# Two PSUM banks for du*B, one for the transposes, three slots of h, and pair sums only on GpSimd, in a fused Mamba and attention kernel

## What is computed

```python
x = whitening of the four channel groups                       # L0, folded into one 128x128 matrix m0
# L1: Mamba block. Per image, L = 1024 positions, 256 inner channels d, 16 states n
delta = softplus(dt @ W_dt + b_dt)
h_t = h_{t-1} * exp(delta_t * A[d, n]) + (delta_t * u_t)[d] * B_t[n]
y_t = sum_n h_t[d, n] * C_t[n];   y = (y + xc * Dp) * silu(z);   x = y @ W_out + x
# L2: attention with softmax over 1024 positions, out = gamma * (v @ softmax(q.k)) + x
# L3: a second softmax attention on theta and phi, convolution, batch norm over all images, + x
```

## Time and profile before

| | us |
|---|---|
| median of 3 runs | 5648.49 |
| lowest and highest | 5642.84, 5652.95 |
| the profiled execution | 5654.98 |
| its span | 5653.2 |

### The profile page before, as it was taken

The page is one execution under the profiler, slowest core; times in us unless marked ns, Lnnn a source line. Parts: engine busy times, 40 slices in busy tenths (PEclk is TensorE's granted clock), DMA queues, the critical chain, the costliest instruction groups (busy, mean ns, idle before and its releaser), DMA issues.

```text
span 5653.2 us, 61917 instructions
## 1 busy us (share of the span) xinstructions
PE 4649.7 (82%) x17331; PEld 2705.2 (48%) x17331; DVE 5067.2 (90%) x5978; ACT 3709.2 (66%) x6077; POOL 4724.3 (84%) x3342
## 2 busy tenths in 40 slices
PE   6568888888888888888888888888888888888871
PEld 6135554455445444545444455445445544554450
DVE  4699999999999999999999999999999999999933
ACT  3456677667766766676677667766666776677633
POOL 0698999999989889898989998989889899999910
PEclk9689999999999999999999999999999999999995
DMA  4456656655655565555556665665566566656517
GB/s 132 176 224 224 224 208 223 229 222 216 224 224 215 215 225 217 216 219 225 223 207 224 224 225 217 222 220 212 219 224 223 210 221 229 224 208 224 219 74 301
DMA packets 199100, 1216.87 MB, mean 215 GB/s; under 512 B 27881, under 2 KB 28657, under 8 KB 67697
## 3 DMA queue, kind: packets, MB, share of 16 engines
q1 hardware_dynamic: 194416, 1196.26, 57.4%
q10 hardware_dynamic: 4352, 16.78, 0.7%
HBM read 1158.43 MB, written 54.53 MB: 215 GB/s over the span
## 4 chain that ended last, share of the span: by engine, by line
PE 38%; DVE 22%; ACT 14%; issue 13%; POOL 10%; DMA 1%; DVEq 0%; SPq 0%; POOLq 0%; ACTq 0%
PE psA L814 13%; PE psE L814 11%; DVE hs L488 8%; DVE psD L484 7%; PE psT L814 7%; POOL pa L300 5%; PE psT L987 4%; ACT da L680 4%; ACT p L726 3%; DVE nm L513 3%; PE psY L814 2%; POOL pa L306 2%; POOL pa L310 1%; ACT L649 1%; ACT pt L690 1%
## 5 line engine op out<-in xcount | busy, mean ns | idle before, releaser
L300 POOL TENSOR_TENSOR pa<-hs,rows_all 128x1024 f32<-128x1024 f32 x1024 | 2412.8, 2356 | 396.8 <-DVE hs L488 396.5
L680 ACT ACTIVATE da<-delta,neg_a 128x512 f32<-128x512 f32 x2048 | 1382.1, 719 | 288.3 <-DVE hs L488 276.2
L484 DVE TENSOR_TENSOR psD<-rows_all,psU 128x512 f32<-128x512 f32 x2048 | 1416.5, 692 | 84.7 <-POOL hlast L304 6.3
L306 POOL TENSOR_TENSOR pa<-pa 128x512 f32<-128x512 f32 x1024 | 1317.1, 1286 | 40.2
L488 DVE TENSOR_TENSOR_SCAN hs<-da,hlast,psD 128x512 f32<-128x512 f32 x1024 | 1310.9, 1280 | 36.3
L488 DVE TENSOR_TENSOR_SCAN hs<-da,psD 128x512 f32<-128x512 f32 x1024 | 1249.4, 1220 | 35.2
L814 PE MATMUL psA<-pt,va 128*128 128x256 f32 x4096 | 989.5, 391 | 71.2 <-DVE x L531 43.7
L814 PEld LDWEIGHTS psA<-pt,va 128*128 128x128 f32 x4096 | 770.0, 194 | 295.5 <-DVE x L531 77.1
L513 DVE TENSOR_REDUCE nm<-psE 128x1 f32<-128x1024 f32 x512 | 620.1, 1211 | 201.1 <-PE psE L814 198.8
L726 ACT ACTIVATE p<-psE,nm 128x1024 f32<-128x1024 f32 x512 | 571.5, 1116 | 316.8 <-DVE nm L513 316.7
L690 ACT ACTIVATE pt<-psT 128x512 f32<-128x512 f32 x1024 | 555.5, 596 | 304.4 <-PE psT L987 301.0
(11 more groups left out here) (186 smaller groups left out, 5017.6 us busy)
## 6 DMA issues: line engine op xcount, KB each, us to landing
rows_all<-bc_scratch SPq DMA_DIRECT2D x1024, 1024.0 KB, 4.7
xin<-x SPq DMA_DIRECT2D x40, 512.0 KB, 7.7
xres<-x SPq DMA_DIRECT2D x64, 256.0 KB, 6.1
x_scratch<-x SPq DMA_DIRECT2D x32, 512.0 KB, 4.3
f_scratch<-fa SPq DMA_DIRECT2D x32, 512.0 KB, 6.8
xres<-x SPq DMA_DIRECT2D x8, 512.0 KB, 3.6
x1g<-x SPq DMA_DIRECT2D x8, 512.0 KB, 3.7
fa<-x SPq DMA_DIRECT2D x8, 512.0 KB, 3.7
```

The costliest lines, as they stand in the source:

```text
L300: pool.tensor_tensor(pa[:, k % PROD, :, :], hs[:, sl, :, :], rows_all[:, slot, 2:4, :], ALU.mult).then_inc(S["prod"], 1)
L306: pool.tensor_tensor(pa[:, k % PROD, 0, :], pa[:, k % PROD, 0, :], pa[:, k % PROD, 1, :], ALU.add).then_inc(S["pair"], 1)
L484: dve.tensor_tensor(psD[:, :], rows_all[:, slot, j, :], psU[:, :], ALU.mult).then_inc(S["dbu_ok"], 1)
L680: act.activation(da[:, k % 2, j, :], delta[:, h, cols(ch)], ACT.Exp, scale=neg_a[:, h, 2 * q + j:2 * q + j + 1]).then_inc(S["da_ok"], 1)
```

## The change

The diff, cut to its core:
- **psD** has two banks; VectorE does both multiplies of a step, then both scans. The copy to psU moves to the end of the group before (`inputs`).
- **hs** has three slots in place of two; VectorE waits for the product two steps back and not for the one of the step before.
- **GpSimd** stops at the pair. TensorE's `add` sums one pair's block at every step, which is 32 sums per image in place of 16, and GpSimd waits for the sum four steps back.
- **psA** is now the second bank of psT. All transposes, the centring and variance, xi of h=0, and the two pre-activations of delta go through the first bank, four transposes at a time, each four waiting until ScalarE has copied the last; xi of h=1, the rows and the weighing go through the second. The gates z use both in turn, h=1 first.
- The keys go through psE. `project` and `project_values` become `query`, `key` and `values` a step later, and x times m0 (`resx`) is taken out of `residual` and put ahead of its wait.

SP's list is unchanged. Wherever ScalarE reads a bank that moved, its line follows.

```diff
@@ buffers and semaphores
+HRING = 3
-        hs = sb("hs", [128, 2, 2, CH])
+        hs = sb("hs", [128, HRING, 2, CH])
-        psD = ps("psD", [128, CH])
+        psD = ps("psD", [128, 2, CH])
         psT = ps("psT", [128, 2, CH])
-        psA = ps("psA", [128, CH])
+        psA = psT[:, 1, :]
-            hlast_ok=STEPS // 2, prod=STEPS, pair=STEPS, quad=STEPS // 2, quad_mm=STEPS // 2, g_ok=2 * NCH,
+            hlast_ok=STEPS // 2, prod=STEPS, pair=STEPS, sum_mm=STEPS, g_ok=2 * NCH,
-        AT_C, AT_N, AT_X, AT_Z, AT_B, AT_P = 0, 3, (5, 7), 9, 10, 11
+        AT_C, AT_N, AT_X, AT_Z, AT_B, AT_P = 0, 3, (5, 6), 9, 10, 11
@@ GpSimd, products
-                    sl, slot = k % 2, k % RING
+                    sl, slot = (b * STEPS + k) % HRING, k % RING
-                    wait(pool, "quad_mm", b, k // 2 - 1)
+                    wait(pool, "sum_mm", b, k - PROD + 1)
...
-                    if k % 2:
-                        wait(pool, "pair", b, k + 1)
-                        pool.tensor_tensor(pa[:, k % PROD, 0, :], pa[:, (k - 1) % PROD, 0, :], pa[:, k % PROD, 0, :], ALU.add
-                                           ).then_inc(S["quad"], 1)
@@ VectorE: scans becomes inputs, spread_inputs, scan_state
+                def inputs(b, k):
+                    ch, h = divmod(k // PAIRS, NH)
+                    wait(dve, "du_ok", b, k // PAIRS + 1)
+                    wait(dve, "dbu_ok", b, 2 * k)
+                    dve.tensor_copy(psU[:, :], du[:, h, cols(ch)]).then_inc(S["u_ok"], 1)
+                def spread_inputs(b, k):
+                    slot = k % RING
+                    if k % PAIRS == 0:
+                        wait(dve, "u_ok", b, k // PAIRS + 1)
+                    at(dve, f"rl{slot}", (b * (STEPS // RING) + k // RING + 1) * 16)
+                    for j in range(2):
+                        wait(dve, "h_ok", b, 2 * (k - 1) + j + 1)
+                        dve.tensor_tensor(psD[:, j, :], rows_all[:, slot, j, :], psU[:, :], ALU.mult
+                                          ).then_inc(S["dbu_ok"], 1)
-                def scans(b, k, j):
+                def scan_state(b, k, j):
                     if j == 0:
-                        at(dve, f"rl{slot}", (b * (STEPS // RING) + k // RING + 1) * 16)
-                        wait(dve, "prod", b, k - 1)
-                        wait(dve, "hlast_ok", b, min(k - 1, NS))
-                    wait(dve, "h_ok", b, 2 * k + j)
-                    dve.tensor_tensor(psD[:, :], rows_all[:, slot, j, :], psU[:, :], ALU.mult).then_inc(S["dbu_ok"], 1)
+                        wait(dve, "prod", b, k - HRING + 1)
+                        wait(dve, "hlast_ok", b, min(k - HRING + 1, NS))
                     wait(dve, "dbu_ok", b, 2 * k + j + 1)
                     wait(dve, "da_ok", b, 2 * k + j + 1)
-                    dve.tensor_tensor_scan(hs[:, sl, j, :], da[:, sl, j, :], psD[:, :],
+                    dve.tensor_tensor_scan(hs[:, sl, j, :], da[:, k % 2, j, :], psD[:, j, :],
@@ VectorE, image
                             if scan:
-                                scans(b, k, 0)
+                                spread_inputs(b, k)
                             if front_of and r == AT_N:
                                 normed(*front_of)
+                            if scan:
+                                scan_state(b, k, 0)
+                            if scan and k % PAIRS == PAIRS - 1 and (k < STEPS - 1 or more):
+                                inputs(*((b, k + 1) if k < STEPS - 1 else (b + 1, 0)))
...
                             if scan:
-                                scans(b, k, 1)
+                                scan_state(b, k, 1)
@@ ScalarE
-                        for h in range(NH):
-                            wait(act, "z_mm", fb, 2 * fc + h + 1)
+                        for n, h in enumerate((1, 0)):
+                            wait(act, "z_mm", fb, 2 * fc + n + 1)
...
-                    if r == AT_P:
-                        for h in range(NH):
+                    if r in (AT_P, AT_P + 1):
+                        h = r - AT_P
...
                             act.activation(pt[:, i // GT % 2, 4 * q:4 * q + 4, 128 * (t % GT):128 * (t % GT) + 128],
-                                           psT[:, q, :].rearrange("p (j i) -> p j i", j=4), ACT.Copy
+                                           psT[:, 0, :].rearrange("p (j i) -> p j i", j=4), ACT.Copy
...
-                        act.activation(ka[:, :], flat(psT), ACT.Identity, bias=c_bk).then_inc(S["k_ok"], 1)
+                        act.activation(ka[:, :], flat(psE), ACT.Identity, bias=c_bk).then_inc(S["k_ok"], 1)
@@ TensorE
-                    if what == "gates":
+                    if what in ("gates1", "gates0"):
+                        h = int(what == "gates1")
+                        wait(pe, "xi_ok", fb, 2 * fc + 2)
+                        if att and h == 1:
+                            wait(pe, "v_ok", *att["valued"])
+                        if att and h == 0:
...
+                        mm(psT[:, h, :], w_in_t[:, DI + C * h:DI + C * h + C],
...
-                    if what == "steps":
+                    if what in ("steps0", "steps1"):
...
                         else:
+                            wait(pe, "sp_abs", fb, 2 * fc + 1)
+                            wait(pe, "sp_relu", fb, 2 * fc + 1)
+                        mm(psT[:, 0, :], w_dt_t[BCR:BCR + DR, C * h:C * h + C], rows_out[BCR:BCR + DR, :]
+                           ).then_inc(S["dpre_mm"], 1)
...
                     if what == "rows":
                         wait(pe, "xc_ok", fb, 2 * fc + 2)
-                        wait(pe, "xi_ok", fb, 2 * fc + 2)
+                        wait(pe, "z_ok", fb, 2 * fc + 1)
...
-                    if q == 1:
+                    if q == 0:
                         wait(pe, "g_ok", b, group)
-                    if k % 2 == 0:
-                        return
-                    wait(pe, "quad", b, (k + 1) // 2)
-                    mm(psY[:, :], ident[:, :], pa[:, k % PROD, 0, :], start=(q == 1), stop=(q == PAIRS - 1)
-                       ).then_inc(S["quad_mm"], 1)
+                    wait(pe, "pair", b, k + 1)
+                    mm(psY[:, :], ident[:, :], pa[:, k % PROD, 0, :], start=(q == 0), stop=(q == PAIRS - 1)
+                       ).then_inc(S["sum_mm"], 1)
...
-                def turn(a, m, t, front):
+                def turn(a, m, t, q, front):
...
-                    for q in range(2):
-                        wait(pe, "pt_ok", a, 2 * (i - 1) + q + 1)
-                        for j in range(4):
-                            last = pe.transpose(psT[:, q, 128 * j:128 * j + 128],
-                                                p[:, i % 2, (4 * q + j) * 128:(4 * q + j + 1) * 128], ident[:, :])
-                        last.then_inc(S["turn"], 1)
+                    wait(pe, "pt_ok", a, 2 * i + q)
+                    for j in range(4):
+                        last = pe.transpose(psT[:, 0, 128 * j:128 * j + 128],
+                                            p[:, i % 2, (4 * q + j) * 128:(4 * q + j + 1) * 128], ident[:, :])
+                    last.then_inc(S["turn"], 1)
...
                 ORDER = [
                     "centre add variance",
-                    "add energy turn weigh0",
-                    "weigh1 turn add residual",
+                    "add energy turn0 weigh0 turn1",
+                    "weigh1 turn0 resx turn1 add residual",
                     "weigh0 weigh1 add",
                     "inner0 add",
-                    "project add",
-                    "project_values add inner1",
+                    "query inner1 add",
+                    "key values add",
                     "energy add",
-                    "skip0 energy turn add",
-                    "gates add energy_next",
-                    "rows turn add",
-                    "add energy steps weigh0",
-                    "turn weigh1 turn_more skip1 add energy_next",
+                    "skip0 energy turn0 gates1 turn1 add",
+                    "gates0 add energy_next",
+                    "rows turn0 add turn1",
+                    "add energy steps0 weigh0",
+                    "steps1 weigh1 turn0 skip1 turn1 more0 energy_next more1 add",
                     "add",
-                    "weigh0 energy turn add",
-                    "turn weigh1 add energy_next",
+                    "weigh0 energy turn0 add turn1",
+                    "turn0 weigh1 turn1 add energy_next",
                 ]
```

More of the change, by code:

```diff
@@ L640, in front @@
                         h = AT_X.index(r)
-                        wait(act, "quad_mm", fb - 1, NS // 2 * (fc + 1))
+                        wait(act, "sum_mm", fb - 1, NS * (fc + 1))
                         wait(act, "xi_mm", fb, 2 * fc + h + 1)
@@ L846, in st_gram @@
                         blk = turned[q][:, 128 * j:128 * j + 128]
-                        last = mm(psD[:, 0:128], blk, blk, start=start and j == 0, stop=stop and j == 3)
```

(11 more changed lines are left out.)

148 lines of the change are left out of this document (75 added, 73 removed).

## The result

The changed kernel takes 5837.39 us (median of 5 runs, 5836.05 to 5837.9) against 5652.95 us (median of 5, 5642.84 to 5656.37) for the kernel before, timed beside it. The ratio is 1.0329, with a 95% interval of 1.0315 to 1.0343: 3.3% slower. The forecast was 5810. The profiled execution has a span of 5835.3 us, 182.1 more than before.

The account below looks back on a forecast made before the run. It took a chain of energies as the bound: TensorE from energy 17 to 7, then hand-overs. Per image 5.7+2.9-3 = +5.6, 31 images +174, image 0 -20, last attention +4: +158, about 5810 us; range 5700 to 5900 (60%).

Parts of the forecast that it names:

- A: Energy 17 to next energy 7, TensorE-bound: three added sums per half, +2.2 us in the query half, +1.0 in the other.
- B: Energy 7 to 8: unchanged in the query half, 6.14 to 4.44 us (-1.7) in the other.
- C+D: Energy 8 to 11: second four transposes of step 10 wait for the first copy, +0.8 us in each half.
- E: Energy 11 to 13, TensorE work without a pause: hand-overs at step 12 add 0.5 us in each half.
- F: Energy 13 to 14: late last copy of step 12 delays ScalarE's queue, +1.4 us query half, +1.5 other.
- G: Energy 14 to 16: a sum between the two fours of step 14 delays exp 14, +0.8 us in each half.
- H: Energy 16 to 17: the new sum of step 0 fills the wait for the squares, cost 0.
- clock: Stretches at 1.2 GHz in the other half shrink as pauses go or fill: bounds 0 and -3.3, taken as -3 us.
- dpre in two steps is covered by weigh0: Step 12, energy 11 to 13: splitting the pre-activations of delta in two was to cost nothing, hidden behind a weighing.
- Image 0: First image, without attention, GpSimd the bound: 16 adds less, VectorE then having room, -20 us.
- the sum below hardly uses either: VectorE's shorter waits: 13.1 us per image by the trace, 0 by the skill; the forecast total hardly used either.
- Rival 1: VectorE is the bound after all: its saving gives -9 us per image, 5355 us total; chance 9%.

Follow-up runs that it names:

- the best version: Changed kernel with transposes of steps 12 and 15 through psE, exponentials ahead of second copies, GpSimd joining six pairs per half into one sum: 5437.93 us, ratio 0.9607.

## Why the prediction was right, and where it was not

Means over 26 images of the steady state, us; the clock term of the forecast lay over the other half as a whole.

| interval | query half before, after | measured, predicted | other half before, after | measured, predicted |
|---|---|---|---|---|
| A | 28.26, 30.74 | +2.5, +2.2 | 28.31, 29.47 | +1.2, +1.0 |
| B | 4.45, 4.43 | 0, 0 | 6.14, 4.43 | -1.7, -1.7 |
| C+D | 15.71, 16.44 | +0.7, +0.8 | 16.02, 16.43 | +0.4, +0.8 |
| E | 10.79, 11.41 | +0.6, +0.5 | 11.10, 11.40 | +0.3, +0.5 |
| F | 5.89, 7.37 | +1.5, +1.4 | 5.36, 6.86 | +1.5, +1.5 |
| G | 8.55, 9.41 | +0.9, +0.8 | 10.01, 9.44 | -0.6, +0.8 |
| H | 6.26, 5.98 | -0.3, 0 | 6.25, 5.98 | -0.3, 0 |
| clock | | | in the rows above | -3 |
| sum | 79.9, 85.8 | +5.9, +5.7 | 83.2, 84.0 | +0.8, -0.1 |

- **Right**: the path (chain of energies, A bound by TensorE), the place and price of the added sums in A, the late copies that lengthen F and G with their mechanism, and the vanished pause of B. The sum is 6.7 us per image where 5.6 was forecast; from the first row maximum to the last (372.4 to 5524.7 before, 347.1 to 5706.6 after) 207.3 us where 174 was forecast. That the sum comes so near is in part luck, as the next two points show: a clock term too large and a wait left out nearly cancel.
- **Mis-sized, the clock**: -3 was taken, the whole 3.3 us that the mean clock of 0.98 gives at most. Four of the 26 images of before have no fall; they take 161.5 us, and the mean of all is 163.1. So the falls cost 1.6 us per image and not 3. A fall of 3.4 us that began in G made G 1.68 us longer (10.59 for 8.91), but one that began between energies 8 and 10 made C+D only 0.56 longer (16.40 for 15.84). Of the 43 falls in these images 37 lie in the other half, where the forecast put them; they make G -0.6 (8.91 without a fall, mean 10.01).
- **Left out, H at 0**: an image of before without a fall has 6.27 in H of the query half and 6.98 in the other, for 5.98 in both after: -1.3, the wait for GpSimd's quad shown above. Behind a fall in G the quad comes in time and H is 5.92. The prediction saw that GpSimd would post its block earlier and gave it no price. Against images without a fall the intervals changed by +8.3 us (8.6 forecast without the clock term), less 1.6 for the clock. Either half of the change is enough to remove the wait: the pair sums alone do it, and with the quads back in the changed kernel H stays at 5.98.
- **A, +0.4 over both halves**: the sums cost 2.58 in each half, as forecast, but the values' wait for `ka` gave back 0.10 and not 0.35 in the query half (28.16 with the quads back, 28.26 before), and the waits for `ka` and x in the other half 1.42 and not 1.6 (26.89, 28.31).
- **Mis-sized, "dpre in two steps is covered by weigh0" and E +0.5**: free of clock falls E went from 10.43 to 11.40, +0.97 in each half. The missing part is no pause: pieces of work that the forecast moved at no cost got longer, as the rows at the end of this section show.
- **Image 0**: -20 forecast, -25.3 measured, and the reason given, 16 adds less on GpSimd, is worth 10 of them. The sums alone move the first row maximum from 372.4 to 362.4; the changed kernel without the sums has 370.0. Together they give 347.1; with the sums but VectorE's old order it is 367.5, since VectorE then does not feed a faster GpSimd. "VectorE then having room" is the step that fails without the pair of multiplies.
- **The last attention**: +4 forecast; from the last row maximum to the end 128.5 and 128.7: nothing.
- **VectorE**: "the sum below hardly uses either" understates it. The saving is real (336 us busy over 32 images, 10.5 each, and waits beside), and 4.6 us per image, the clock fall in them, reach the time of the changed kernel. As the prediction read the Trainium skill ("VectorE: DVE Perf Modes", The DRAIN you can't avoid), this term was to be 0. That section compares copies with and without semaphores, which no run here does; the run with the old order has the same instructions, each waiting for the one just ahead, and VectorE 336 us busier, so for a change of order the measurement decides. Rival 1 (VectorE the bound) is out for the changed kernel. In the best version VectorE holds back part of the gain, in B of the other half.

TensorE in E of the kernel before, query half, to be set beside its timeline of the changed kernel above:
```profile
2676.53 1.98 PE L814 MATMUL psT<-rows_out,w_dt_t 8*128 8x512 f32 x4
2678.44 1.99 PE L814 MATMUL psA<-pt,va 128*128 128x256 f32 x8
2680.27 1.04 PE L987 MATMUL psT<-ident,p 128*128 128x128 f32 x8
2681.14 1.89 PE L814 MATMUL psA<-pt,va 128*128 128x256 f32 x8
2682.87 0.61 PE L814 MATMUL psA<-ident,rinv 128*128 128x128 f32 x4
```
From start to start, the pre-activations of delta took 1.91 us in one piece and take 1.05 + 1.05; the two weighings took 1.83 + 1.73 and take 1.92 + 1.84. That is 0.2 for each pair, without a wait in those rows, where the 8-row product now comes twice between others. No run undoes this order alone, so that the order is the reason is likely but not shown. The transposes of step 12 up to energy 13 take 0.44 + 1.42 + 0.47 for 1.74: +0.6, near the +0.5 of the forecast.

The total: 207.3 - 25.3 + 0.1 = 182.1 us of span, for +158 forecast.

## What to carry to other kernels

Price added work by the stretch it falls in. A sum cost its full 0.86 us where the engine never paused and less than nothing where it did. So put work into the pauses and take it out of the full stretch; that turned a loss of 0.6% into a gain of 1.4%. When a buffer goes from two banks to one, look less at the producer's pauses than at what stands behind the late copy in the consumer's queue: moving one exponential ahead of it returned 106 us. A scarce bank can be borrowed from a tile that is empty just then, as psE is between an exponential and the next energy; what that alone brings was not timed apart from the other moves. And before a pause is put down to the clock, compare images with and without a fall: here half of what looked like the clock was a wait for another engine.

## What the hardware showed that was not expected

- More work on TensorE made it faster: ten sums per image in its pauses removed all 31 clock falls (3.4 us at 1.2 GHz each) and 1.8 us per image. Which pause brings a fall was not tried.
- A VectorE multiply with one input in PSUM takes 0.69 us beside a busy GpSimd; with both inputs outside PSUM it took 1.64 us on average, and 3.42 us a pair where it met GpSimd's product.
- Where a product of 8 rows stood between products of 128 rows, it and its neighbour took about 0.1 us longer each, without a wait in the trace; this was seen at one place of the kernel and not tested alone.
